# Turning the token tiles, Wk and the context in 32x32 blocks on VectorE, with the layer-norm mean folded into centred weights

## The reference

```python
def xattn(text, features, Wq, bq, Wk, bk):            # text [4,1024,2048], features [4,64,2048]
    Q = einsum('btx,dx->btd', text, Wq) + bq
    K = einsum('bpx,dx->bpd', features, Wk) + bk
    attn = softmax(einsum('btd,bpd->btp', Q, K) / sqrt(2048))
    return einsum('btp,bpd->btd', attn, features)
def ffn(h, Wq, Wr, aux_keys, aux_values, Wvd, Wvu, Wu1, bu1, Wu2, bu2, gate_w1, gate_bias, log_rel):
    query = h @ Wq.T                                   # 64 wide
    scores = (query @ Wr.T) @ (aux_keys @ Wr.T).T / sqrt(48) + log_rel     # 512 slots
    top8 of scores; w = softmax(query . aux_keys[top8] / 8 + log_rel[top8])
    aux_out = (w @ aux_values[top8]) @ Wvd.T @ Wvu.T
    u = clip(0.5 * log1p(var(h)) / mean(log1p(var(h))) + 2.5 * sigmoid(gelu(h @ Wu1.T + bu1) @ Wu2.T + bu2), 0, 5)
    gate = sigmoid(gate_w1 * clip((u - 0.5) / 1.5, 0, 1) + gate_bias); gate = 0 where gate < 0.05
    return h + gate * aux_out
x = x + tanh(g_xattn) * xattn(layernorm(x), ctx, ...)
out = x + tanh(g_ffn) * ffn(layernorm(x), ...)
```

## Time and profile before

| | |
|---|---|
| median of 3 runs | 1187.81 us (1185.8 to 1188.9) |
| the profiled execution: its own time, its span | 1185.06 us, 1183.3 us |
| mean granted TensorE clock | 0.975 |
| busy: PE, DVE, ACT, POOL | 1120.2, 745.7, 451.8, 166.3 us |
| keys, score weights, memory weights, tokens, gates, output | 0 to 140.6, to 257.3, to 302.5, to 991.5, to 1016, to 1183.3 us |

### The profile page before, as it was taken

How to read it: one execution, slowest core, us unless ns; L and a number is a source line. 1 busy time by engine, 2 the same in 40 slices (tenths; PEclk the granted TensorE clock), 3 DMA queues, 4 the chain that set the end, 5 groups by cost and what they waited for, 6 DMA issues and landing times. The chain is left out here.

```text
span 1183.3 us, 20524 instructions
## 1 busy us (share of the span) xinstructions
PE 1120.2 (95%) x7402; PEld 1067.6 (90%) x7402; DVE 745.7 (63%) x1891; ACT 451.8 (38%) x743; POOL 166.3 (14%) x272
## 2 busy tenths in 40 slices
PE   7999979799899999999999999999999997699998
PEld 6999979787899999999999999999999996477876
DVE  6555665446426666666766676766666665688786
ACT  3333324335213343343334343334334333455553
POOL 0000230000001212121222212121212212000000
PEclk9999989899899999999999999999999998799999
DMA  7334448877418721320111411113201014799997
GB/s 268 131 138 142 138 128 300 234 267 283 107 61 214 186 65 71 106 88 36 71 35 51 143 38 69 35 71 106 88 35 71 35 72 146 247 382 422 424 424 335
DMA packets 114650, 185.32 MB, mean 157 GB/s; under 512 B 45876, under 2 KB 95060, under 8 KB 97624
## 3 DMA queue, kind: packets, MB, share of 16 engines
q1 hardware_dynamic: 109432, 147.11, 37.2%
q10 hardware_dynamic: 4608, 33.56, 6.8%
q0 software_dynamic: 576, 4.19, 0.8%
HBM read 140.55 MB, written 54.79 MB: 165 GB/s over the span
## 5 line engine op out<-in xcount | busy, mean ns | idle before, releaser
L47 PE MATMUL tk_hidden_sum<-b_weights,k_turned 128*128 128x384 f32 x512 | 180.0, 352 | 0.0
L49 PE MATMUL tk_hidden_sum<-b_weights,k_turned 128*128 128x384 f32 x512 | 172.4, 337 | 0.0
L48 PE MATMUL tk_hidden_sum<-b_weights,k_turned 128*128 128x384 f32 x512 | 171.5, 335 | 0.0
L47 PE MATMUL tk_b_sum<-b_weights,k_turned 128*128 128x320 f32 (+1 forms) x528 | 166.3, 315 | 0.0
L49 PE MATMUL tk_b_sum<-b_weights,k_turned 128*128 128x320 f32 (+1 forms) x528 | 163.8, 310 | 0.0
L48 PE MATMUL tk_b_sum<-b_weights,k_turned 128*128 128x320 f32 (+1 forms) x528 | 163.4, 309 | 0.0
L965 ACT ACTIVATE k_turned<-tk_bank 128x512 fp32r<-128x512 f32 x128 | 76.4, 598 | 202.9 <-PE tk_bank L77 185.1
L1132 DVE TENSOR_TENSOR k_turned<-tk_bank,k_turned 128x512 fp32r<-128x512 f32 x128 | 88.3, 691 | 66.0 <-ACT k_turned L965 65.6
L47 PEld LDWEIGHTS tk_b_sum<-b_weights,k_turned 128*128 128x128 f32 x528 | 99.2, 188 | 0.3
L48 PEld LDWEIGHTS tk_b_sum<-b_weights,k_turned 128*128 128x128 f32 x528 | 99.3, 188 | 0.0
L49 PEld LDWEIGHTS tk_b_sum<-b_weights,k_turned 128*128 128x128 f32 x528 | 99.1, 188 | 0.0
(11 more groups left out here) (263 smaller groups left out, 2602.5 us busy)
## 6 DMA issues: line engine op xcount, KB each, us to landing
k_rows<-in_x_dram SPq DMA_DIRECT2D x48, 1024.0 KB, 4.9
k_rows<-in_Wk_dram SPq DMA_DIRECT2D x16, 1024.0 KB, 4.8
k_rows<-in_Wq_dram SPq DMA_DIRECT2D x16, 1024.0 KB, 6.2
late_x<-in_x_dram SPq DMA_DIRECT2D x16, 1024.0 KB, 13.4
out_dram<-k_rows ACTq DMA_DIRECT2D x16, 1024.0 KB, 10.2
out_dram<-late_x ACTq DMA_DIRECT2D x16, 1024.0 KB, 10.4
b_weights<-scratch_b SPq DMA_DIRECT2D x6, 1024.0 KB, 6.5
scratch_mt<-k_way_out SPq DMA_DIRECT2D x32, 128.0 KB, 1.9
```

The source lines that it names most:

```text
L47: pe.matmul(out, lh, rh, start=start, stop=False, skip_group_check=skip)
L48: pe.matmul(out, lh, rl, start=False, stop=False, skip_group_check=skip)
L49: return pe.matmul(out, ll, rh, start=False, stop=stop, skip_group_check=skip)
```

## The change

- x, Wk and the context are turned by DVE (`dve.transpose`, 32x32 blocks) from SBUF into the PSUM banks that PE wrote before. For this they are loaded with `load_in_blocks`: four DMAs of 256 KB, each to 32 partitions, in pieces of 2 KB. Wk and the context are read by DVE in dense runs of 32 elements; x is read with a step of 16 elements (64 B).
- x is not centred any more. The mean is taken out of the weights instead: rows of Wq, of the memory layer's Wq and of Wu1 are centred (ACT: a pass that sums, a tiny one, a pass that subtracts), and the low part of Wq subtracts the mean too. Mean and variance of the tokens come from a second, plain copy of x, by two passes of ACT (`row_sum`, `squares`) and POOL.
- Wq is loaded in whole rows and is the stationary operand as it lies; the score weights of all 16 chunks are summed in 8 PSUM banks over 16 steps and split and stored (4 MB) at the end.
- The centred context comes from a second turn by PE (8 groups with a step of 16 elements) in the last two Wk tiles, and one POOL operation is left of two.
- In the token loop `late_z` and the turned slot weights move one tile later.

```diff
 def transpose_group(pe, bank, src, g, ident, rows=P, spread=False):
+        part = slice(c, D, KC) if spread else slice(c * P, (c + 1) * P)
+def load_in_blocks(sp, src, n, dst, done):
+    view = src.rearrange("(t k j) (q f) -> t q j k f", k=P // LANES, j=LANES, q=QUADS)
+    for q in range(QUADS):
+        sp.dma_start(dst[q * LANES:(q + 1) * LANES, :].rearrange("j (k f) -> j k f", f=QN),
+                     view[bass.ds(n, 1), q].rearrange("o j k f -> (o j) k f")).then_inc(done, 16)
+def turn_blocks(dve, bank, src, g):
+    return dve.transpose(bank[:].rearrange("p (c k j) -> p c k j", c=4, j=LANES),
+                         src[:].rearrange("p (k c i) -> p c k i", k=P // LANES, i=LANES)[:, 4 * g:4 * g + 4])
 # keys_block, DVE
             def body(j, last=False):
                 for u in range(2):
                     if not (last and u == 1):
                         parts_lo(2 * j + u + 1, 1 - u)
+                    if not last:
+                        turn_weights(j + 1, u)
                     key_parts(2 * j + u, u)
 # ffn_block, ACT, before the jobs 4, 5, 8, 9, 10
+            def centre(n):
+                act.activation(own[0:r, :], own[0:r, :], ACT.Copy, accum_out=row_sum[0:r, :])
+                act.activation(row_nmean[0:r, :], row_sum[0:r, :], ACT.Copy, scale=-1.0 / D)
+                act.activation(own[0:r, :], own[0:r, :], ACT.Identity,
+                               bias=row_nmean[0:r, 0:1]).then_inc(centred, 1)
 # token_block, SP
+        def load_tile(sp, t):
+            sp.wait_ge(S["turned"], G * t)
+            load_in_blocks(sp, io["x"], t, keep["blocks"], keep["blocks_in"])
+            sp.wait_ge(S["squares"], t)
+            load_rows(sp, io, keep, t)
 # token_block, PE
                 a_part(t, u, 0, first)
-                if not last:
-                    pe.wait_ge(S["centred"], t + 2)
-                    turn_x(t + 1, 1 - u, 0)
                 a_part(t, u, 1, first)
-                if not last:
-                    turn_x(t + 1, 1 - u, 1)
 # token_block, DVE
+            def turn_x(t, g):
+                dve.transpose(bank[g % 2][:].rearrange("p (c k j) -> p c k j", c=4, j=LANES),
+                              blocks[:].rearrange("p (k i c) -> p c k i", k=P // LANES, c=KC)[:, 4 * g:4 * g + 4]
+                              ).then_inc(S["turned"], 1)
 # token_block, ACT
+            def row_sum(t, u):
+                act.activation(plain[:], plain[:], ACT.Copy, accum_out=rsum[u][:]).then_inc(S["row_sum"], 1)
+            def squares(t, u):
+                act.activation(plain[:], plain[:], ACT.Square, bias=mv[u][:, 0:1], scale=-1.0,
+                               accum_out=rsq[u][:]).then_inc(S["squares"], 1)
```

More of the change, by code:

```diff
@@ L150, in _, with plain_turn @@
         def _(pe):
[L151 to L163, removed]
+            def plain_turn(n):
+                if n:
+                    pe.wait_ge(plain_out, n)
+                transpose_group(pe, plain_ps, crow[n // GROUPS], n % GROUPS, ident, spread=True).then_inc(plain_turned, 1)
             def body(j, first=False, last=False):
@@ L176, in body @@
                             ins.then_inc(product, 1)
[L177 to L183, removed]
+                        if last:
+                            plain_turn(GROUPS * u + g)
+            pe.wait_ge(ident_done, 2)
+            pe.wait_ge(small_in, 16 * 7)
+            pe.transpose(ps_bias[:, 0:2 * KC], raw[:], ident[0:2 * KC, 0:2 * KC]).then_inc(bias_turned, 1)
             body(0, first=True)
+            with pe.Fori(1, KC // 2 - 1) as j:
+                body(j)
             pe.wait_ge(diag_done, 2)
@@ L239, in _, with turn, turn_weights @@
         def _(dve):
+            def turn(src, n):
+                for g in range(GROUPS):
+                    turn_blocks(dve, bank[g], src, g).then_inc(turned, 1)
+            def turn_weights(j, u):
+                dve.drain()
+                dve.wait_ge(rows_in[u], 16 * QUADS * (j + 1))
+                turn(rows[u], 2 * j + u)
             def parts_lo(n, u):
@@ L388, in _, with row_sum @@
[L388 to L396 removed]
+            def row_sum(n):
+                wq_sum(act, keep, n).then_inc(row_summed, 1)
@@ L445, in ffn_jobs @@
+            step(KC - 1, 1, last=True)
 def ffn_jobs(io):
@@ L1027, in context_hi @@
                 act.activation(cw_hi[r], cw[r], ACT.Copy).then_inc(S["cw_high"], 1)
-            for t in range(2):
-                centre(t, t)
+            row_sum(0, 0)
+            squares(0, 0)
             context_hi(0)
@@ L1277, in gates, with tile @@
                 op(dve.tensor_scalar, keep["f_att"][:], keep["f_x"][:], tgx[:, 0:1], None, ALU.mult)
-            def tile(t, u, j, late=True, last=False, ahead=True, first=False, second=False):
+            def tile(t, u, j, late=True, late_z_too=True, last=False, first=False, second=False):
                 if late:
```

645 lines of the change are left out of this document (356 added, 289 removed).

## The result

The changed kernel takes 1169.42 us (median of 4 runs, 1167.04 to 1172.1), the kernel before beside it 1187.09 us: ratio 0.9851, 95% interval 0.9825 to 0.9877. It is faster by 18 us, where 42 were forecast. The profiled execution took 1167.04 us, its span is 1165.2 us, at a mean clock of 0.961.

| stage | before | after | change | forecast |
|---|---|---|---|---|
| keys | 0 to 140.6 | 0 to 154.1 | +13.5 | +8 |
| score weights | to 257.3 | to 263.6 | -7.2 | -16 |
| memory weights | to 302.5 | to 323.7 | +14.9 | +23 |
| context products, tile 0 | to 365.3 | to 396.5 | +10.0 | -3.6 |
| the other 31 tiles | to 991.0 | to 969.1 | -53.1 | -54.0 |

The account below looks back on a forecast made before the run. PE was taken as bound in token loop and keys. Against 1185.1 us: keys +8, score weights -16, memory weights +23, loop -57.6, gates +0.6 give 1143, or 1146 as median; range 1120 to 1182, with 62% for 1130 to 1165.

Parts of the forecast that it names:

- T: Unknown price of one DVE transpose: 0.64 us taken for dense Wk, 0.64 to 1.07 us carried for x.
- The rivals that needed 1.22 us: DVE transposes: two passes at 1.22 us, 1188 us in all, 7%; or dearer still, 1214 to 1314 us, 9%.
- an order of DVE that holds PE up in every tile: Token loop: reading the blocks waits for POOL, 1 us a tile, 32 us, total 1178 us; 10%.
- The cheap rival: Memory weights cost less, half of the centring hidden, and keys cost nothing: minus 20, total 1126 us; 12%.
- Token loop, minus 57.6 us: PE loses 4 transpose groups in each of 32 tiles, 128 x 0.45 us; DVE and loads stay hidden.
- Keys, plus 8: Keys stage: DVE becomes the bound; 4 us gained over 14 Wk tiles, against later start, context moments and second turn.
- plus 2: Last Wk tile: PE waits for ACT's copies of the second turn of the context, 2 us.
- Score weights, minus 16: 16 steps of 5.71 us on PE, plus start and end: 100.5 us against 116.7.
- plus 3: End of the score weights: the PSUM banks are emptied behind the last step, 3 us.
- plus 6: Start of the score weights: a 9 us POOL operation holds DVE up and the clock is low, 6 us.
- Memory weights, plus 23: Centring, 4.6 us on ACT for 5 jobs, makes ACT the chain: plus 20, and 3 for low clock.
- Output, 0: Output stage: the same loads and products, so no change in time.

Follow-up runs that it names:

- t2: Changed kernel with SP issuing the load of tile 1 ahead of the stores of the second context product: 1163.44 us, ratio 0.9796.
- t7: Changed kernel with tile 1's load earlier, tile 0's attention ahead of turns of tile 1, and POOL's deviation of tile 1 after tile 0's statistics: 1162.62 us, 0.9784.
- c1: Changed kernel with Wk and context turned by PE as before, centred context made by DVE, and first token tile reordered: 1152.92 us, ratio 0.9706.
- k4: Changed kernel without the second turn of the context in the last two Wk tiles (output not the reference's): 1164.46 us, ratio 0.9803.
- k1: Changed kernel with Wk and context loaded in plain rows and turned by PE as before, second turn kept: 1162.34 us, ratio 0.9789.
- s3: Changed kernel with ACT's high part of Wq tile 1 earlier and the centred context made by DVE in two halves, not POOL: 1167.11 us, ratio 0.9836.
- s2: Changed kernel with four of the eight closing score-weight stores issued by POOL instead of SP: 1174.46 us, ratio 0.9895.
- s4: Changed kernel with the last four score-weight stores issued by SP first thing in the next block: 1170.72 us, ratio 0.9876.
- f1: Changed kernel without ACT's two full centring passes on the memory layer's Wq and Wu1 (output not the reference's): 1156.1 us, ratio 0.974.
- t1: Changed kernel with tile 0's attention weights (ACT and DVE) made ahead of the turns of tile 1: 1169.55 us, ratio 0.9843.

## Where the prediction was right and where it was wrong

- **T.** Right for the dense case (0.61 apart in a row, 0.64 taken), and x came out at the upper end carried (1.07), from a row that bears it only in part. The rivals that needed 1.22 us, or an order of DVE that holds PE up in every tile, fell: no transpose of x took over 1.12 us, although POOL is busy for 151 us of the loop. The cheap rival had half of the centring hidden, where about a third was, and keys at nothing, where they cost 13.5.
- **Token loop, minus 57.6 us: the step that failed.** "PE loses 4 groups in each of 32 tiles" holds for the steady tiles (-53.1 against -54.0). It was applied to tile 0 too, by "the blocks of a tile can be loaded once its predecessor is turned", which is a sentence about the steady loop. At its start the load stands in SP's queue behind a store that waits for DVE, and it serves one buffer where before two tiles were ahead. +10.0 instead of -3.6, more than half of what is missing: PE waits 9.2 us once, and the clock behind it is low. t2 showed 6 of the 13.6 us to be the place of that load, t7 and c1 have up to 2 more, and the rest is open.
- **Keys, plus 8.** The turns by DVE cost 6.1 as forecast; "plus 2" for the second turn of the context was mis-sized, it is 6.6 to 7.4 (k4, k1). I had counted PE's wait for ACT and not PE's own 8 groups, nor the waits on both sides of the Wq row tile (4.1 and 2.3 us). The later start was mis-sized too (8.0 for 4.5), by DVE's wait of 4.7 us for the second block of the context, and DVE's shorter tile paid for it.
- **Score weights, minus 16.** The steps stand 5.76 us apart (5.71 forecast). Of the 8.8 us that are missing, 3.8 are the end (6.8 us from PE's last matmul to the next stage, "plus 3"), 2.6 are PE idle between 208 and 226, when ACT waits for Wq while the stores of the centred context are under way (no run separates the two), 0.8 the steps, and about 2 the start (what is left of the 109.5 us is about 8, with 5.3 us of wait and then a clock of 0.69; "plus 6"). s3 shortens the stage by 3 us, by taking POOL from DVE's way; of the end s2 and s4 get nothing back.
- **Memory weights, plus 23.** The mechanism was right and its price too high: centring costs 13.3 to 14.4 us (f1), the clock behind it included, where 20 and then 3 for the clock had been taken. This error of 8 us has the other sign.
- **Output, 0.** It takes 3.1 us more with the same instructions. Neighbouring matmuls of 512 columns stand 0.234 us apart after and 0.227 before, at a clock of 1.00 in both. It is no accident of one execution: in the 18 of the changed kernel and its variants the stage takes 168.7 to 172.8 us, against 166.5 in the one of the kernel before. The cause stays open; no run tried it.
- **Sum.** 13.6 + 8.8 + 5.5 + 3.1 + 0.9 + 0.1 - 8.1 = 23.9 us, the difference of -42 and -18.1. The range (1120 to 1182) holds the time; the likeliest case (1130 to 1165) does not. That the time came so near is in part luck: the memory weights cost 8 us less than forecast, and without that the gain would have been 10 us.

## What to carry to other kernels

A gain per iteration is to be multiplied by the iterations that are steady; the first ones are walked through, queue by queue, with the landing time of each first load. Where a wait is removed at a border between stages, look at the engines' orders for the next one before pricing it: in t1 the wait of 9.2 us went and one of 9.8 stood behind it. What is moved to an engine with spare time costs nothing only in the loop that has that spare time; the same turn was hidden in the token loop and cost 6 us in keys, so the best version takes the one and leaves the other.

## What the runs showed of the hardware that I had not expected

- DVE's operation with two operands in SBUF does not slow down beside POOL's operation on whole tensors, it stops: 9.79 us instead of 2.35. DVE's operations on 128x1 went on meanwhile (0.15 us each at 156.15 and 158.04 in the changed kernel, where POOL works from 154.20 to 163.20), and so did the transposes of x in the loop (1.015 to 1.115 us).
- A block whose last DMA is issued from POOL's queue ended 8.4 us after that issue was over (s2, 263.4 to 271.7); with SP's queue it is 0.4 us (263.2 to 263.6).
- The same code stands ahead of it, yet the score weights start between 154.1 and 157.3 us in thirteen profiled executions of the changed kernel and its variants. A stage border in one execution is good to some 3 us, which is why the terms above are read beside the ratios.
